# An attention kernel on one core: two maxima and part of the last block's work go to VectorE, the sums leave PSUM as one product, and one tile of a block changes engine

## The reference

```
scores = leaky_relu(x @ ks.T, 0.2)
scores = where(adj > 0, scores, -9e15)
attn   = softmax(scores, axis=1)
out    = layernorm(x + attn @ ks)      # over the 128 columns, eps 1e-5
```

## Time and profile before

| | us |
|---|---|
| three timed runs, median (lowest to highest) | 1552.17 (1549.71 to 1552.98) |
| the profiled execution | 1553.51 |
| its span in the profile | 1551.4 |
| PE busy in the span | 1509.1 |
| DVE | 1501.4 |
| ACT | 1480.0 |
| POOL | 1440.4 |

### The profile page before, as it was taken

The page is one execution under the profiler, slowest core; times in us unless marked ns, Lnnn a source line. Parts: engine busy times, 40 slices in busy tenths (PEclk is TensorE's granted clock), DMA queues, the critical chain, the costliest instruction groups (busy, mean ns, idle before and its releaser), DMA issues.

```text
span 1551.4 us, 43381 instructions
## 1 busy us (share of the span) xinstructions
PE 1509.1 (97%) x16828; PEld 1419.9 (92%) x16828; DVE 1501.4 (97%) x1808; ACT 1480.0 (95%) x1887; POOL 1440.4 (93%) x1246
## 2 busy tenths in 40 slices
PE   6699999999999999999999999999999999999997
PEld 5499999999999999999999999999999999999987
DVE  6999999999999999999999999999999999999984
ACT  6999999999999999999999999999999999999997
POOL 4999999999999999999999999999999999999996
PEclk8999999999999999999999999999999999999999
DMA  9865656555556655566665555655655655555610
GB/s 352 271 200 191 197 198 203 196 188 195 194 191 190 202 189 196 192 191 196 199 192 191 188 188 188 200 183 188 194 189 189 201 185 189 193 188 189 197 63 8
DMA packets 107131, 296.00 MB, mean 191 GB/s; under 512 B 10800, under 2 KB 40240, under 8 KB 106928
## 3 DMA queue, kind: packets, MB, share of 16 engines
q1 hardware_dynamic: 106928, 293.25, 57.6%
HBM read 289.01 MB, written 4.19 MB: 189 GB/s over the span
## 4 chain that ended last, share of the span: by engine, by line
PE 70%; issue 11%; DVE 9%; ACT 7%; POOL 3%; DVEq 0%; DMA 0%; ACTq 0%; POOLq 0%
PE weighted L806 20%; PE scores L758 10%; PE scores L760 10%; PE scores L759 10%; PE weighted L822 6%; PE weighted L818 6%; PE weighted L820 6%; DVE ring L680 3%; ACT ring L493 3%; DVE running L664 3%; ACT pt_hi L500 2%; DVE ring L650 1%; POOL pt_lo L401 1%; POOL kt_lo L363 1%; ACT xt_hi L468 1%
## 5 line engine op out<-in xcount | busy, mean ns | idle before, releaser
L396 POOL TENSOR_TENSOR ring<-ring,floor 128x768 f32<-128x768 f32 (+1 forms) x498 | 706.2, 1418 | 49.2 <-ACT floor L520 49.2
L401 POOL TENSOR_TENSOR pt_lo<-ring,pt_hi 128x512 f16<-128x512 f32 (+1 forms) x512 | 659.5, 1288 | 17.7 <-ACT pt_hi L500 17.2
L650 DVE SCALAR_TENSOR_TENSOR ring<-adj_sb,scores 128x1024 f32<-128x1024 int32 x512 | 620.2, 1211 | 6.8 <-ACT scores L486 6.4
L486 ACT ACTIVATE scores<-scores,shrink 128x1024 f32<-128x1024 f32 x512 | 553.8, 1082 | 51.5 <-PE scores L760 47.0
L493 ACT ACTIVATE ring<-ring,lift 128x1024 f32<-128x1024 f32 x512 | 583.6, 1140 | 1.6 <-POOL ring L396 1.2
L758 PE MATMUL scores<-xt_hi,kt_hi 128*128 128x256 f16 x2048 | 559.8, 273 | 22.8 <-DVE ring L650 15.2
L760 PE MATMUL scores<-xt_hi,kt_lo 128*128 128x256 f16 x2048 | 560.4, 274 | 0.0
L759 PE MATMUL scores<-xt_lo,kt_hi 128*128 128x256 f16 x2048 | 560.1, 273 | 0.0
L664 DVE TENSOR_TENSOR running<-ring,running 128x1024 f32<-128x1024 f32 x448 | 547.2, 1221 | 0.1
L806 PE MATMUL weighted<-k_rows,ring 128*128 128x129 f32 x3472 | 471.6, 276 | 2.0 <-DVE y L701 1.0
L806 PEld LDWEIGHTS weighted<-k_rows,ring 128*128 128x128 f32 x3472 | 426.6, 192 | 14.1 <-ACT ring L493 8.2
(11 more groups left out here) (76 smaller groups left out, 559.2 us busy)
## 6 DMA issues: line engine op xcount, KB each, us to landing
adj_sb<-in_adj SPq DMA_DIRECT2D x512, 512.0 KB, 3.4
ring<-in_ks_t SPq DMA_DIRECT2D x8, 512.0 KB, 7.3
x_row<-in_x SPq DMA_DIRECT2D x32, 128.0 KB, 3.6
out<-normed SPq DMA_DIRECT2D x32, 128.0 KB, 3.6
x_probe<-in_x_t SPq DMA_DIRECT2D x29, 128.0 KB, 3.5
xt_raw<-in_x_t SPq DMA_DIRECT2D x29, 128.0 KB, 4.4
ring<-in_ks SPq DMA_DIRECT2D x12, 128.0 KB, 7.4
k_rows<-in_ks SPq DMA_DIRECT2D x12, 128.0 KB, 3.8
```

Of the source, the lines that this page charges most:

```text
L396: nc.gpsimd.tensor_tensor(here, here, below, ALU.subtract).then_inc(gap_ready, 1)
L401: nc.gpsimd.tensor_tensor(pt_lo[:, g % PARTS, 0:QUAD - whole, :], ring[:, g % RING, whole:, :], pt_hi[:, g % PARTS, 0:QUAD - whole, :], AL ...
L650: nc.vector.scalar_tensor_tensor(ring[:, g % RING, :, :], adj_sb[:, g % ADJS, :, :], 0.0, scores[:, g % 2, :, :], ALU.is_le, ALU.subtract)\
```

## The change

What it does, in five parts:

- The maxima of steps 6 and 7 of `ks_t` go from ScalarE's `bound_ks_t` to VectorE's `magnitude`, ahead of masks 4 and 5; ScalarE splits units 3 to 7 one slot earlier and takes the bounds of steps 4 and 5 later.
- VectorE divides the sums by the denominator straight out of PSUM: `recip` of the ones column, then one product `ratio` (both sides, 256 elements) into SBUF. TensorE's next block waits for `ratio_ready`. The residual reads `ratio` from SBUF, with the scale taken back by `unscale_rows`, and moves to the end of the slot. The slot's first gap moves ahead of `finish`.
- VectorE subtracts 27 tiles of a block: one tile for q = 0, 4, 8, 11, 12, else two.
- In the drain VectorE subtracts all tiles of the last 18 groups and three of the two before, reading the last block's floors when TensorE has them (`spread_ready`); ScalarE's floor copy of that block goes.
- VectorE makes the fp16 high parts of the last 8 groups and normalises the last block.

```
-    MAGNITUDES = (2, 4, 6, 7, 8, 9)
+    MAGNITUDES = (2, 4, 8, 9, 10, 11)
-    LEFT_OUT = GROUPS - 2
+    LEFT_OUT = GROUPS + 2
+    LAST_HIGHS = 8
...
-            return QUAD if g >= ALL - LEFT_OUT else 3 if g >= ALL - GROUPS else min(1 + g % 4, 2)
+            return QUAD if g >= ALL - LEFT_OUT else 3 if g >= ALL - LEFT_OUT - 2 else 1 if g % GROUPS in (0, 4, 8, 11, 12) else 2
+
+        def wait_high(eng, g):
+
+            if g < ALL - LAST_HIGHS:
+                eng.wait_ge(part_hi_ready, g + 1)
+            else:
+                eng.wait_ge(dve_hi_ready, g + 1 - (ALL - LAST_HIGHS))
...
                 nc.gpsimd.tensor_tensor(rstd[:, :], var[:, :], minus_half[:, :], ALU.pow).then_inc(rstd_ready, 1)
+                if b == BLOCKS - 1:
+                    return
...
-                if g is not None:
+                if g is not None and g < ALL - LAST_HIGHS:
                     high_part(g)
...
-                if 3 <= s < 6:
-                    bound_ks_t(s + 2, s)
-                if s < 8:
+                if s == 0:
+                    split_ks_t(2)
+                if s == 5:
+                    bound_ks_t(5, 3)
+                elif s < 5:
+                    split_ks_t(s + 3)
+                elif s < 8:
                     split_ks_t(s + 2)
-                if s == 1:
+                if s == 3:
                     bound_ks_t(4, 2)
...
-                b = whole_late(s, AT_SPREAD, 1)
-                if b is not None:
+                b = whole(s, AT_SPREAD)
+                if b is not None and b < BLOCKS - 1:
                     spread(b)
...
-                    if b is not None:
+                    if b is not None and b < BLOCKS - 1:
                         normalise(b, j)
...
-                dve.wait_ge(floor_ready, b + 1)
+                if b == BLOCKS - 1:
+                    dve.wait_ge(spread_ready, b + 1)
+                else:
+                    dve.wait_ge(floor_ready, b + 1)
...
             def finish(b):
-                at = b % 2
+
                 total = sums(b)[:, 0:SIDES * LANES].rearrange("p (j w) -> p j w", j=SIDES)
                 dve.wait_ge(weighted_ready, GROUPS * (b + 1))
-                nc.vector.tensor_scalar(denom[:, :], total[:, :, ONES], scale_rows, None, ALU.mult).then_inc(denom_ready, 1)
-                dve.wait_ge(denom_ready, b + 1)
+                wait(dve, ratio_ready, b)
+                nc.vector.reciprocal(recip[:, :], total[:, :, ONES]).then_inc(recip_ready, 1)
+                dve.wait_ge(recip_ready, b + 1)
                 wait(dve, y_ready, SIDES * b)
-                nc.vector.reciprocal(recip[:, :], denom[:, :]).then_inc(recip_ready, 1)
+                nc.vector.tensor_tensor(ratio[:, :, :], total[:, :, 0:D],
+                                        recip[:, :].unsqueeze(2).to_broadcast([P, SIDES, D]), ALU.mult)\
+                    .then_inc(ratio_ready, 1)
+
+            def residual(b):
+                at = b % 2
+                dve.wait_ge(ratio_ready, b + 1)
                 dve.wait_ge(xrow_loaded[at], 16 * (b // 2 + 1))
-                dve.wait_ge(recip_ready, b + 1)
                 wait(dve, normed_ready, SIDES * b)
                 for j in range(SIDES):
-                    nc.vector.scalar_tensor_tensor(y[:, j, :], total[:, j, 0:D], recip[:, j:j + 1],
-                                                   x_row[:, at, j, :], ALU.mult, ALU.add,
-                                                   accum_out=y_sum[:, j:j + 1]).then_inc(y_ready, 1)
+                    nc.vector.scalar_tensor_tensor(y[:, j, :], ratio[:, j, :], unscale_rows, x_row[:, at, j, :],
+                                                   ALU.mult, ALU.add, accum_out=y_sum[:, j:j + 1]).then_inc(y_ready, 1)
+
+            def high_part(g):
+
+                dve.wait_ge(prob_ready, g + 1)
+                dve.wait_ge(weighted_ready, g + 1 - PARTS)
+                whole = WHOLE[g % GROUPS]
+                nc.vector.tensor_copy(pt_hi[:, g % PARTS, 0:QUAD - whole, :], ring[:, g % RING, whole:, :])\
+                    .then_inc(dve_hi_ready, 1)
+
+            def normalise(b):
+
+                dve.wait_ge(normed_ready, SIDES * b)
+                dve.wait_ge(out_stored[b % 2], 16 * (b // 2))
+                dve.wait_ge(rstd_ready, b + 1)
+                for j in range(SIDES):
+                    nc.vector.tensor_scalar(normed[:, b % 2, j, :], y[:, j, :], neg_mean[:, j:j + 1], rstd[:, j:j + 1],
+                                            ALU.add, ALU.mult).then_inc(normed_ready, 1)
 
             for s in SLOTS:
-                b = whole(s, AT_FINISH)
-                if b is not None:
-                    finish(b)
+                if 4 <= s < 6:
+                    dve.wait_ge(ks_t_loaded[s + 2], 16)
+                    magnitude(mag_k[:, s + 2:s + 3], ks_t_raw[:, (s + 2) * STEP:(s + 3) * STEP])
                 if s == 6:
                     most(2)
+                ended = whole(s, AT_FINISH)
+                if ended is not None:
+                    if ended < BLOCKS - 1:
+                        gap(s - AT_GAP + 1)
+                    finish(ended)
+                    if ended == BLOCKS - 1:
+                        residual(ended)
                 g = group(s, 0)
                 if g is not None:
                     mask(g)
+                g = group(s, AT_PART)
+                if g is not None and g >= ALL - LAST_HIGHS:
+                    high_part(g)
+                if whole(s, AT_NORMALISE[0]) == BLOCKS - 1:
+                    normalise(BLOCKS - 1)
...
-                    if g is not None and early == (g % GROUPS > 0):
+                    if g is not None and early == (g % GROUPS > 0) and (ended is None or ended == BLOCKS - 1):
                         gap(g)
...
+                if ended is not None and ended < BLOCKS - 1:
+                    residual(ended)
...
-                    wait(pe, y_ready, SIDES * b)
+                    wait(pe, ratio_ready, b)
...
-                pe.wait_ge(part_hi_ready, g + 1)
+                wait_high(pe, g)
                 pe.wait_ge(part_lo_ready, g + 1)
```

More of the change, by code:

```diff
@@ L100, in adj_attention_layernorm @@
         lift = sb("lift", [P, 1], F32)
-        denom = sb("denom", [P, SIDES], F32)
+        ratio = sb("ratio", [P, SIDES, D], F32)
         xt_raw = sb("xt_raw", [P, 3, BLOCK], F32)
@@ L173, in adj_attention_layernorm @@
         dve_gap_ready = sem("dve_gap_ready")
+        dve_hi_ready = sem("dve_hi_ready")
         part_hi_ready = sem("part_hi_ready")
         part_lo_ready = sem("part_lo_ready")
-        denom_ready = sem("denom_ready")
+        ratio_ready = sem("ratio_ready")
         prob_ready = sem("prob_ready")
@@ L230, in adj_attention_layernorm @@
         scale_rows = f32_column(scale, K_ALL)
+        unscale_rows = f32_column(unscale, K_ALL)
         def scales_there(stage):
@@ L398, in low_part @@
             def low_part(g):
-                pool.wait_ge(part_hi_ready, g + 1)
+                wait_high(pool, g)
                 whole = WHOLE[g % GROUPS]
@@ L716, in _ @@
                 if s == 5:
-                    dve.wait_ge(mag_k_bounded, 6)
+                    dve.wait_ge(mag_k_bounded, 4)
+                    dve.wait_ge(mag_step, 6)
                     magnitude(mag[:, K_SETS[2]:K_SETS[2] + 1], mag_k[:, CUTS[2]:CUTS[3]])
```

## The result

The changed kernel takes 1568.30 us (median of 4 runs, 1566.13 to 1568.49), the kernel before 1551.47 (4 runs, 1549.71 to 1552.98): a ratio of 1.0103, 95% interval 1.0091 to 1.0115. Forecast were 1550.1 us and a range up to 1561.

A forecast was written before the change was run, and what follows sets the result against it. The prediction took TensorE and VectorE as level bounds, each waiting for the other once a block. From 1552.17 us, head -2.4, drain -4.6 and steady state +4.9 gave 1550.1 us, range 1536 to 1561.

The forecast's parts named there:

- (g): Middle blocks, first `least`: VectorE gets the port 0.13 us before GpSimd's `low_part` 13; period 46.69 us against 46.48, +0.21.
- rival C: First `least` of each block waits 1.04 us behind `low_part` 13: period 47.21, +0.73, total 1565 us; chance 0.22.
- the cycle: Middle blocks: timing loop from first `least` through residual and GpSimd's queue to the next first `least`, 46.69 us.
- (a) to (c): VectorE's block work: a tile fewer -0.27, `ratio` for `denom` +0.07, a gap covering the 0.24 wait; 46.04 us.
- (e): Middle blocks: GpSimd gets a tile more in one of its gaps, a step of 0.53 us.
- (f): Residual moves behind slot 38's mask and `least`, 13.23 us after the first `least`; `mean` starts 0.72 us behind the residual's start.
- (d): Block change: TensorE waits for `ratio_ready`, some 0.4 us ahead of the old `y_ready`; its 0.26 us stall goes.
- The residual blocked by `low_part` 1: Middle blocks: VectorE's residual, with two SBUF operands, waits 0.65 us for GpSimd's `low_part` 1.
- Signs to look for: Profile marks named beforehand for middle blocks: period 46.7 us and `low_part` 13 at about 2.0 if the forecast is right.
- The head, -2.4: Kernel start: mask 6 at 30.9 us instead of 33.25, a gain of 2.4 us, ends -1 and -4.
- The drain, -4.6: Kernel end: earlier exponentials -1.4, fewer ScalarE waits -1.1, last groups -1.6, final steps -0.5; ends -2 and -6.5.
- A: Middle blocks: engine sums hold and TensorE streams at 46.22 us a block, -7.8 us, total 1537.4; chance 0.22.

The follow-up runs named there:

- experiment 5: The changed kernel with GpSimd's `mean` and ScalarE's first `squares_of` each one slot later: 1596.0 us, ratio 1.0287 to the kernel before.
- Experiment 7: The kernel before with the changed head and drain, its column of ones scaled so that `denom` goes, 28 tiles: 1539.81 us, ratio 0.9918.
- experiment 4: The changed kernel's head and drain around the block body of the kernel before, 28 tiles: 1547.64 us, ratio 0.9972.

## Why the prediction was wrong

The step that failed is (g), "VectorE wins by 0.13", and with it the range, which left rival C throughout outside. The mechanism, the place and the price were in the text; the order of the two at the port was not what I took it for. VectorE does come first, by 0.16 us (674.38 against 674.54 for `low_part` 13), as the cycle said. But gap 15 holds the port until 674.44, a term that the cycle left out, and when it lets go `low_part` 13 gets by: `least` waits 1.18 us in each block. Rival C thus came true without the condition that I gave it, GpSimd earlier or VectorE later by 0.13.

- **Taken from the wrong pair.** From the earlier trace rows I read that a `least` gets the port 0.13 us ahead of GpSimd's recorded end. In both pairs there nothing was queued right behind: the next GpSimd instruction came 0.89 and 0.09 us later. In the middle block gap 15 is followed at once by `low_part` 13. In the changed kernel and the three with tiny operations there are 100 such meetings, with `least` asking 0.05 to 0.43 us ahead of the release. It lost all 100, each time by its lead plus 1.10 to 1.13 us, the whole of the next instruction; four more that asked up to 0.06 after the release lost as well, and so did the 14 `shrink`s. Where the next GpSimd record began at least 0.08 us after the end (some 160 cases over all traces, residual ops among them), it waited its lead and no more. In experiment 5 a residual op got in first, in 29 cases with a lead of 1.25 to 1.39 us and in one with 0.04.
- **The forecast and rival C were 1% apart in the sum (1550.1 and 1565), and 0.13 us apart in the cause.** I gave C 0.22. A cycle that turns on 0.13 us should have had its two ends at like weight, and the range up to 1565 or more.
- **C's working stands.** The residual to the next `least`: 32.81 forecast, 674.38 - 641.58 = 32.80 measured. The residual to `low_part` 13: 32.94 and 674.54 - 641.58 = 32.96. The first `least` to the residual less the wait: 13.23 and 14.35 - 1.18 = 13.17. VectorE's own work: 46.04 and 47.15 - 1.18 = 45.97. Period of C: 47.21 and 47.15 to 47.16. Terms (a) to (c), (e) and (f), taken together, were thus right within 0.1 us.
- **(d), TensorE's stall goes:** wrong for the kernel as a whole. VectorE comes so late that TensorE waits 0.7 us for `ratio` in each block (17.5 us in 26). Experiment 7 shows what was to be had, 46.23.
- **The residual blocked by `low_part` 1, 0.65 us:** not so, it took 0.34. With `least` served late, GpSimd is past that `low_part` and idle at `mean` (0.97 us). Experiment 5 shows the contention as soon as that idle time is gone.
- **Signs to look for:** "`least` at 2.2 us" (2.40) was named for C, and its period of 47.21; `neg_mean` released by y was right. The idle time before GpSimd's first gap went (40.2 us in 200 to 1400 before, 3.3 after), as under both.
- **The head, -2.4:** mask 6 at 30.9 was forecast, 31.04 measured; but the earlier trace rows came from an execution in which the clock was 0.50 in 28 to 32 us, and the old head has mask 6 at 31.22 where it is 1.00. Undone alone the head is worth about 1.4. The term was taken from one execution, and its gain didn't last to mask 23 in full. That the clock makes the difference is the reading that fits three executions of the old head; no run changes the clock alone.
- **The drain, -4.6:** 4.1 in spans (4.6 in experiment 4). Head and drain together are worth 3.9 in timed medians, against 7.0 forecast. Of the drain's own steps, the copy: VectorE's cast of 512 elements took 0.47, a step of 0.40 where I took 0.6. The copies do meet GpSimd at the port, as the sum allowed for: the first of the eight took 0.94 and the last 1.41, where the same shapes take 0.47 and 0.62.
- **A slip in the rivals:** half of A's 7.8 us gives 1541, not 1544. Nothing else was built on it.

VectorE's timeline in the drain of the changed kernel:

```profile
1544.29 0.47 DVE L734 CAST pt_hi<-ring 128x512 f16<-128x512 f32 x1
1544.69 1.21 DVE L699 TENSOR_TENSOR ring<-ring,floors 128x1024 f32<-128x1024 f32 x1
...
1547.34 0.62 DVE L734 CAST pt_hi<-ring 128x768 f16<-128x768 f32 x1
1547.88 1.21 DVE L699 TENSOR_TENSOR ring<-ring,floors 128x1024 f32<-128x1024 f32 x1
```

From 512 to 768 elements the step grows by 0.14 us, 0.55 ns an element; between the gaps of 512 and 1024 it grows from 0.59 to 1.13, 1.05 ns an element. The Trainium skill, page "VectorE: DVE Perf Modes", section "The perf-mode tier table", gives such a copy twice the rate of the 1x ops, and the trace agrees for the rate. The step of 0.40 lies above the 0.3 that I worked out from it.

The Trainium skill, page "SBUF — State Buffer", section "Who interferes with whom", has the later to issue wait for the whole other instruction. The traces agree for a single one, and show more: the 100 `least`s waited for the rest of the instruction running and for the whole next one too.

## What to carry to other kernels

- Before an instruction is moved towards another engine's queue, look at what stands right behind the instruction that it will meet. Here the shared port passed to the next in that queue in 118 of 148 such meetings, whether VectorE had asked long before or not, so the price is the rest of one instruction or the rest and a whole one more.
- When a forecast turns on a tenth of a microsecond, both outcomes belong in the range. Here the price of losing was 1.1 us in each block.
- Ask first which engine's own work is the floor. The best case of this change was 0.26 us a block, the stall of TensorE; one scale moved into a constant column got it, with no new pair of SBUF operands on VectorE.

## What the runs showed of the hardware

- In all 118 meetings in which GpSimd ran a two-tile gap (128 x 512) with a `low_part` right behind, the VectorE instruction that asked meanwhile (`least` with two SBUF operands, or `shrink`) lost to the second of them too, with leads from 1.14 us before the release to 0.06 after it. In the 30 in which GpSimd ran a three-tile gap and VectorE a residual op, with leads of 0.04 and of 1.25 to 1.39, VectorE went ahead of the `low_part`, and that took 0.05 to 0.08 us more. What decides between the two is open; the lead alone doesn't.
- Two VectorE instructions in a row with two SBUF operands each ask anew: the first waited 1.3 us, the second 0.9 (experiment 5).
- A wait for the port stands inside the record of the waiting instruction. VectorE's busy share rose from 97 to 98% while its own work fell from 46.24 to 45.97 us a block.
